# GRU inputs read back from DRAM in pairs of steps and turned by VectorE in blocks, instead of turned group by group by TensorE

## The reference

```
# layer 0, attention over T = 32, 16 heads of 16
scale, shift = split(cond @ W_emb + b_emb)
xn  = rms_norm(x, g_norm) * (1 + scale) + shift
q, k, v = heads(xn @ W_qkv);  q, k = rms_norm(q, g_q), rms_norm(k, g_k)
o   = softmax(q k^T / 4) v
x2  = x + o + o @ W_out
# layer 1, GRU over time, first state h = cond
gi = x2[:, t] @ W_ih + b_ih;  gh = h @ W_hh + b_hh
r, z = sigmoid(gi_r + gh_r), sigmoid(gi_z + gh_z)
n = tanh(gi_n + r * gh_n);  h = (1 - z) * n + z * h
out[:, t] = x2[:, t] + h
```

## Time and profile before

| | |
|---|---|
| median of 3 runs | 342.4 us (342.23, 342.4, 343.04) |
| span of the profiled execution | 340.0 us |
| busy: PE, DVE, ACT, POOL | 323.3, 246.3, 238.0, 224.5 us |
| attention, then seam, then GRU | to about 180, 180 to 195, from 195 us |
| granted TensorE clock | 1.00 in all slices |

### The profile page before, as it was taken

The page is one execution under the profiler, slowest core; times in us unless marked ns, Lnnn a source line. Parts: engine busy times, 40 slices in busy tenths (PEclk is TensorE's granted clock), DMA queues, the critical chain, the costliest instruction groups (busy, mean ns, idle before and its releaser), DMA issues.

```text
span 340.0 us, 12168 instructions
## 1 busy us (share of the span) xinstructions
PE 323.3 (95%) x4177; PEld 293.4 (86%) x4177; DVE 246.3 (72%) x665; ACT 238.0 (70%) x722; POOL 224.5 (66%) x404
## 2 busy tenths in 40 slices
PE   8988899899999999999986999999999999999994
PEld 8767788788888888888874999999999999999994
DVE  3778898888999999999996455565555556555555
ACT  4787777778888788889656566666666666666662
POOL 6787787867777877878778346555555555555542
PEclk9999999999999999999999999999999999999999
DMA  5965237742343333233332221111112111122221
GB/s 202 307 193 151 86 76 234 226 132 85 109 121 113 101 114 99 86 117 116 112 109 65 80 77 48 61 49 62 62 62 62 48 58 50 62 62 62 63 62 33
DMA packets 32205, 34.14 MB, mean 100 GB/s; under 512 B 5286, under 2 KB 26796, under 8 KB 32172
## 3 DMA queue, kind: packets, MB, share of 16 engines
q1 hardware_dynamic: 25868, 26.10, 25.6%
q10 hardware_dynamic: 6304, 7.61, 7.0%
HBM read 12.46 MB, written 8.39 MB: 61 GB/s over the span
## 4 chain that ended last, share of the span: by engine, by line
PE 78%; POOL 7%; SPq 4%; DMA 4%; issue 3%; DVE 3%; ACT 1%; POOLq 0%; DVEq 0%; ACTq 0%
PE bank L1287 38%; PE bank L1244 19%; PE bank L1400 4%; PE bank L1419 4%; PE bank L1388 4%; DMA operands<-operands 4%; PE bank L1531 3%; SPq L414 2%; POOL operands L485 2%; PE bank L1380 2%; SPq L405 2%; PE bank L1250 2%; PE bank L1371 2%; POOL xn L496 1%; POOL xn_lo L531 1%
## 5 line engine op out<-in xcount | busy, mean ns | idle before, releaser
L1287 PE MATMUL bank<-wih_lo,wo_parts 128*128 128x256 f32 x192 | 56.2, 294 | 0.0
L1287 PE MATMUL bank<-wih_hi,wo_parts 128*128 128x256 f32 x192 | 54.6, 285 | 0.2 <-POOL pair_lo L600 0.2
L1287 PE MATMUL bank<-wih_hi,pair_lo 128*128 128x256 f32 x192 | 52.8, 279 | 0.0
L1287 PE MATMUL bank<-wqkv_hi,hT_hi 128*128 128x256 f32 x192 | 52.5, 292 | 0.0
L611 POOL TENSOR_TENSOR operands<-operands,h 128x128 f32<-128x128 f32 x64 | 29.6, 462 | 34.2 <-ACT operands L932 33.4
L1287 PE MATMUL bank<-wqkv_lo,hT_hi 128*128 128x256 f32 x192 | 49.9, 279 | 0.0
L1187 DVE TENSOR_TENSOR operands<-bank,operands 128x128 f32<-128x128 f32 x64 | 18.6, 291 | 39.3 <-ACT operands L929 39.3
L1244 PE MATMUL bank<-wqkv_hi,xn_hi 128*128 128x512 f32 (+1 forms) x124 | 46.4, 375 | 0.2 <-POOL xn_lo L531 0.2
L618 POOL TENSOR_TENSOR w_emb_sb<-h,w_emb_sb 128x256 f32<-128x256 f32 x31 | 22.9, 737 | 30.7 <-DVE h L1204 30.7
L1287 PE MATMUL bank<-wqkv_hi,hT_lo 128*128 128x256 f32 x192 | 42.7, 279 | 0.0
L1244 PE MATMUL bank<-wqkv_hi,xn_lo 128*128 128x512 f32 (+1 forms) x124 | 41.9, 338 | 0.0
(11 more groups left out here) (138 smaller groups left out, 975.2 us busy)
## 6 DMA issues: line engine op xcount, KB each, us to landing
v_diag<-v_rows SPq DMA_DIRECT2D x124, 34.0 KB, 2.1
operands<-operands SPq DMA_DIRECT2D x32, 128.0 KB, 2.1
out_dram<-x ACTq DMA_DIRECT2D x16, 256.0 KB, 2.6
w_emb_sb<-out_dram SPq DMA_DIRECT2D x32, 128.0 KB, 2.1
operands<-operands SPq DMA_DIRECT2D x63, 64.0 KB, 2.0
out_dram<-w_emb_sb SPq DMA_DIRECT2D x31, 128.0 KB, 1.7
x_in<-in_x_dram SPq DMA_DIRECT2D x7, 512.0 KB, 8.6
stage_w<-in_L_cond_W_ih_dram ACTq DMA_DIRECT2D x2, 384.0 KB, 3.4
```

The costliest lines, as they stand in the source:

```text
L1287: return pe.matmul(dst, moved, gate_columns(weights, k, block), start=False, stop=True, skip_group_check=True)
```

## The change: what it does, and the diff

Only groups 24 to 31 are still turned by TensorE, and only their first two steps are kept (`late_x2T`, 4 x 32 columns). Everything else comes back from DRAM: for each pair of steps SyncE issues four DMAs, one for each quarter of the features, that put x2 with the group on 32 partitions of each quarter (`load_quarters`; runs of 64 features, 256 bytes). VectorE turns the 128x512 tile in 32x32 blocks (`turned_quarters`), even and odd features apart, and GpSimd makes the high and low parts from it, its reads being strided now (`turned_pair`). The features so come in another order, and the rows of w_ih are loaded in that order. The weights' tile is no longer shared by pair_hi. The last two groups are stored by SyncE instead of ScalarE. For pair 0 the quarters of groups 0 to 23 are loaded ahead of the end of attention.

```diff
+FIRST_TURNED = 24
-        x2T = sb("x2T", [P, KC * T * B])
+        late_x2T = sb("late_x2T", [P, 2 * KC, NTURNED * GB])
+        x_quarters = sb("x_quarters", [P, 2, 2 * D])
+        x_turned = sb("x_turned", [P, 2, 2 * D])
+        def turned_pair(slot):
+            return x_turned[:, slot, :].rearrange("p (i n g) -> p n g i", i=GB, n=2 * KC)
+        def by_parity(slot):
+            return x_quarters[:, slot, :].rearrange("p (n f c) -> p n c f", n=2 * GB, c=KC)
 # SyncE
+            def load_quarters(pair, slot, groups):
+                n = 2 * pair
+                rows = out[groups.start * GB:groups.stop * GB, bass.ds(n, 2), :]
+                for f in range(4):
+                    sp.dma_start(x_quarters[PB * f + groups.start:PB * f + groups.stop, slot, :],
+                                 rows[:, :, f * QF:f * QF + QF]).then_inc(quarters_loaded[slot], 16)
+            for stored in x2_stored:
+                sp.wait_ge(stored, 16 * (NG // 4 - early_stores))
+            load_quarters(0, 0, early)
+            sp.wait_ge(x2_ready, NG)
+            sp.dma_start(out.rearrange("(g b) t d -> (b t) g d", b=GB)[:, NG - 2:NG, :], x2[:, 2:4, :])\
+              .then_inc(x2_stored[1], 16)
             for stored in x2_stored:
                 sp.wait_ge(stored, 16 * (NG // 4))
+            def next_quarters(pair, slot):
+                sp.wait_ge(quarters_turned, pair - 1)
+                load_quarters(pair, slot, slice(0, NG))
+            load_quarters(1, 1, slice(0, NG))
+            load_rows(0, 0)
+            load_rows(1, 1)
+            next_quarters(2, 0)
...
 # GpSimd
-            pool.wait_ge(x2T_ready, NG)
+            pool.wait_ge(quarters_turned, 1)
+            pool.tensor_copy(by_group(pair_hi[:, 0, :, :])[:, :, early, :], turned_pair(0)[:, :, early, :])\
+                .then_inc(early_high, 1)
...
             def high_pair(u, slot):
-                pool.tensor_copy(pair_hi[:, slot, :, :], x2T_pair(u)).then_inc(pair_hi_ready, 1)
+                pool.wait_ge(quarters_turned, u + 1)
+                pool.tensor_copy(by_group(pair_hi[:, slot, :, :]), turned_pair(slot)).then_inc(pair_hi_ready, 1)
 # ScalarE
-                    result(d)
+                    if later(d, FIRST_TURNED) and isinstance(d, int):
+                        result(d)
+                rows = source[(i % KC) * P:(i % KC) * P + P, :]
+                if i < KC:
+                    rows = source.rearrange("(f c) n -> c f n", c=KC)[i]
 # VectorE
+                if turn_is(base, u, NG - 1 + DVE_PT):
+                    dve.wait_ge(quarters_loaded[0], 64)
+                    dve.transpose(x_turned[:, 0, :], by_parity(0)).then_inc(quarters_turned, 1)
...
+            def turned_quarters(pair, slot, loads):
+                dve.wait_ge(quarters_loaded[slot], 64 * loads)
+                if later(pair, 3):
+                    dve.wait_ge(pair_lo_ready, pair - 1)
+                dve.transpose(x_turned[:, slot, :], by_parity(slot)).then_inc(quarters_turned, 1)
             # in step, ahead of reset_state(0):
+                if isinstance(t, int) and t == 0:
+                    turned_quarters(1, 1, 1)
+                if s % 2 == 1 and has_pair(base, (s + 3) // 2):
...
 # TensorE
-                if d is not None and not late_result:
+                if isinstance(d, int) and d >= FIRST_TURNED and not late_result:
                     result_transposes(d, (u - PE_X2T) % 4)
...
+            pe.wait_ge(early_high, 1)
             pe.wait_ge(first_pair_hi, 1)
```

More of the change, by code:

```diff
@@ L261, in adaptive_attention_gru @@
         x2T_ready = sem("x2T_ready")
+        quarters_clear = sem("quarters_clear")
+        quarters_loaded = [sem(f"quarters_loaded{i}") for i in range(2)]
+        quarters_turned = sem("quarters_turned")
+        early_high = sem("early_high")
+        early_low = sem("early_low")
         rz_ps = [sem(f"rz_ps{c}") for c in range(KC)]
@@ L346, in has_pair, with by_group @@
             return not isinstance(base, int) or base // 2 + n < T // 2
[L348 to L352, removed]
+        early, late, last_group = slice(0, FIRST_TURNED), slice(FIRST_TURNED * GB, B - GB), slice(B - GB, B)
+        late_rows, last_rows = slice(0, (NTURNED - 1) * GB), slice((NTURNED - 1) * GB, NTURNED * GB)
+        def turned_pair(slot):
+            return x_turned[:, slot, :].rearrange("p (i n g) -> p n g i", i=GB, n=2 * KC)
+        def by_parity(slot):
+            return x_quarters[:, slot, :].rearrange("p (n f c) -> p n c f", n=2 * GB, c=KC)
+        def by_group(pair):
+            return pair.rearrange("p n (g i) -> p n g i", i=GB)
         turn = [0]
@@ L446, in store_rows, with rows @@
                 sp.dma_start(out[:, t, :], x2_rows[:, s, :]).then_inc(out_done[s], 16)
-            def rows(q, s):
+            def next_quarters(pair, slot):
+                sp.wait_ge(quarters_turned, pair - 1)
+                load_quarters(pair, slot, slice(0, NG))
+            def rows(q, s, quarters=True):
                 store_rows(q * 4 + s, s)
@@ L453, in rows @@
                     load_rows(q * 4 + s + 2, (s + 2) % 4)
-            for t in range(4):
-                load_rows(t, t)
+                if isinstance(q, int) and q == 0 and s == 0:
+                    next_quarters(3, 1)
+                if quarters and s % 2 == 1:
+                    next_quarters(q * 2 + (s + 7) // 2, (s + 7) // 2 % 2)
+            load_quarters(1, 1, slice(0, NG))
+            load_rows(0, 0)
+            load_rows(1, 1)
+            next_quarters(2, 0)
+            load_rows(2, 2)
+            load_rows(3, 3)
             for s in range(4):
                 rows(0, s)
-            with sp.Fori(1, T // 4 - 1) as q:
+            with sp.Fori(1, T // 4 - 2) as q:
                 for s in range(4):
                     rows(q, s)
+            for s in range(4):
+                rows(T // 4 - 2, s, False)
             for s in range(2):
-                rows(T // 4 - 1, s)
+                rows(T // 4 - 1, s, False)
             store_rows(T - 2, 2)
@@ L1098, in residual @@
                 if later(o, 4):
-                    dve.wait_ge(x2T_ps, o - 3)
+                    if isinstance(o, int) and o >= FIRST_TURNED + 4:
+                        dve.wait_ge(x2T_ps, o - 3 - FIRST_TURNED)
                     dve.wait_ge(x2_stored[slot // 2], (o - slot) * 4)
@@ L1304, in input_term @@
                 part, weights = ((pair_hi, wih_hi), (pair_hi, wih_lo), (pair_lo, wih_hi))[term]
-                return add_product(input_block(e, block), part[:, pair_slot, k, e * B:e * B + B], weights, k, block)
+                return add_product(input_block(e, block), part[:, pair_slot, e * KC + k, :], weights, k, block)
             def unread_products(tiles, count):
@@ L1376, in result_transposes @@
                 pe.wait_ge(v_ready, capped(d, PE_X2T - PE_V + (1 if isinstance(d, int) and d in LATE_RESULTS else 0)))
-                if later(d, 1):
-                    pe.wait_ge(x2T_ready, d)
+                if d > FIRST_TURNED:
+                    pe.wait_ge(x2T_ready, d - FIRST_TURNED)
                 for c in range(KC):
-                    last = pe.transpose(p_x2T[:, c * P:c * P + P], x2[:, slot, c * P:c * P + P], ident[:, :])
+                    last = pe.transpose(p_x2T[:, c * P:c * P + P],
+                                        x2[:, slot, :].rearrange("p (f c) -> p c f", c=KC)[:, c], ident[:, :])
                 last.then_inc(x2T_ps, 1)
```

61 lines of the change are left out of this document (36 added, 25 removed).

## The result

The changed kernel takes 352.28 us (median of 4 runs, 351.68 to 353.52) against 342.31 us before: a ratio of 1.0295, 95% interval 1.0267 to 1.0323. It is slower, as predicted, but by twice the amount: the forecast was 347.0 us, and the measured time lies above the upper end of the range, 349.8. A second set of 6 runs on another chip gave 350.21 us and 1.0245 (1.0195 to 1.0295), its median just over that end too. The profiled execution took 351.68 us with a span of 349.9 us. One execution of the kernel before (440.88 us), one of experiment 5 (357.58 us) and one of the repeat of experiment 6 (354.41 us, the profiled one) ran over 1.5% longer than the fastest of their kernel at a lower granted clock, and no median, ratio or reading here uses them.

The account below looks back on a forecast made before the run. TensorE was taken as the bound, with 78% of the chain of waits. Span 340.0 - 3.7 (attention) + 1.0 and 5.8 (seam) + 1.6 (clock) = 344.7 us, plus 2.4 to the median, taken as 347.0 us; range 343.0 to 349.8.

Parts of the forecast that it names:

- it can grow by 0.7 us unseen: Steady GRU: GpSimd's low part of 1.30 us, followed by z*h, could lengthen by 0.7 us at no cost.
- the steady GRU: GRU steps behind the seam: block transposes, more DMAs and strided reads cost nothing, within 0.2 us.
- GpSimd pays for strides: Rival, chance 0.05: GRU low parts at double cost make z*h 0.5 us late per pair, 7.5 us; 356 us.
- The seam, first place: Turn of the pair 0 blocks ahead of oT(30), behind the quarters' loads: +1.0 us, ends 0 and 2.
- the sum: Whole kernel: 340.0 - 3.7 + 1.0 + 5.8 + 1.6 = 344.7 us of span; median 347.1, taken as 347.0 us.
- Attention: Removed result transposes shorten turns that TensorE sets by 0.22 us: gain 3.7 us, ends 3.3 and 5.3.
- VectorE becomes the bound: Rival, chance 0.07: in attention VectorE's 4.72 us of work leave 0.11, half of the gain goes; 349 us.
- Step 0: Seam, second place: GRU step 0 waits for the last store, then pair 1's loads: +5.8 us, ends 4.3 and 7.
- The clock: TensorE, idle near 6 us before h, restarts step 1 at half pace: +1.6 us, ends 0 and 3.3.
- Clock kept: Rival, chance 0.30: the same seam, but TensorE's clock does not fall; 345.4 us.
- Not slower: Rival, chance 0.12: ahead of step 0, pair 1's quarters are in by 195.4 us; 341.4 us.

Follow-up runs that it names:

- experiment 5: Changed kernel with pair 0 turned after oT(31), pairs 1 and 2 turned in steps 1 and 2, and strides on VectorE's write: 345.41 us, 1.0055.
- experiment 6: Changed kernel with 36 unread products on TensorE ahead of its wait for h(0): 349.58 us, 1.0272; on the other chip 349.19 us, 1.0220.
- experiment 3: Changed kernel with the strides moved from GpSimd's reads to VectorE's transpose write: 348.51 us, 1.0179.
- experiment 4: Kernel before, with GpSimd's high and low parts of pairs 1 and up reading in strides of 256 bytes, nothing else: 345.51 us, 1.0136.
- experiment 1: Changed kernel with VectorE's block transpose of pair 0 behind oT(31) instead of ahead of oT(30): 351.01 us, 1.0266.
- experiment 8: Changed kernel with the 24 pairs of result transposes of groups 0 to 23 back on TensorE, unread: 355.35 us, 1.0441.
- experiment 2: Changed kernel with the turn and the high and low parts of pairs 1 and 2 one step later: 352.67 us, 1.0284.
- 10: Changed kernel with pairs 0 and 1 made early, strides on VectorE's write, and pair 1's turn and parts moved later: 338.68 us, 0.9892.

## Why the prediction was wrong

**The step that failed:** "it can grow by 0.7 us unseen", of GpSimd's low part in the steady GRU. I had checked it against z*h of the next step alone. Its first reader is TensorE, which wants it for the next inputs ahead of h; there the slack is next to nothing already in the kernel before. So the term that I had at nothing, the steady GRU, was +2.38 us. The growth itself was in my rival "GpSimd pays for strides", with the wrong reader and so the wrong price (half a microsecond over a bound of 0.7, 7.5 us in all, chance 0.05). Measured: 1.30 us became 1.58, +22%, the copy 0.61 became 1.13, +84%, and the steady steps lost 2.4 us; with plain reads (experiment 3) that loss was gone, and with strides alone (experiment 4) it was there. The Trainium skill (GPSIMD Engine Reference, 7. Performance pitfalls for Q7 kernels) gives such reads 50% more. Here the copy had 84% and the subtraction 22%, so the measurement decides.

**The seam, first place:** right mechanism, mis-sized, +2.15 us against +1.0. Counted from scores 31, oT(30) came 2.98 us later (the wait of 2.27 and the transpose of 0.71), where I had 2.0: the four issues took 3.40 us, where I had taken the 2.84 of the earlier trace rows, and landed about 1 us later than I had it. The slack behind it was 0.8 us, near the 1.0 of the sum. Experiment 1 took 1.96 us away.

**Attention:** right mechanism, mis-sized: -2.56 us in this profile against -3.7. Of the 1.1 us that are missing, 0.64 are the late start of this profile, which is chance and no effect of the change. The other 0.5 lie up to turn 15, where scores waited 1.40 and 1.42 us for keys and I had let half of the gain through; from there to scores 31 the gain was 3.48 us, against my 3.5. The mean over ten profiles is -3.0, and single ones differ by 3 us. The rival "VectorE becomes the bound" is out: a turn of 4.85 us is what TensorE's slots give (5.05 less 0.22 is 4.83), VectorE has 0.12 us to spare in it, and with the transposes back (experiment 8) the turn is 5.06 us again.

**Step 0:** right, +6.29 against +5.8, by the steps I had named: store, four loads, block transpose, high and low part, z*h. The strides took 0.45 + 0.22 us of it, where I had 0.3.

**The clock:** right, +1.59 against +1.6, and shown by experiment 6. The Trainium skill (TensorE: Matmul & The Clock Gate, HAM oscillation) describes a TensorE that waits for DMAs and comes back at half clock. This trace agrees, with 0.50 behind a wait of 6.18 us for h, which stood behind DMAs. "Clock kept" is out.

**The sum:** the four misses are 2.4 + 1.15 + 1.1 + 0.5 = 5.2 us; 347.0 + 5.2 = 352.2 against 352.28. All went to the same side. Without the 0.64 us of chance in attention's the kernel would still lie above the range. "Not slower" fell where I had put its point of decision: the quarters of pair 1 landed at 196.9 us (197.3 in the old trace's frame, by residual 31), not by 195.4.

## What to carry to other kernels

When an operation on a side engine grows, list every reader of its result and take the earliest one in program order; a multiplication issued half a step ahead is easily missed, and moving work to "one step later" fails for the same reason. Where a transposed or regrouped tile must be strided on one side, put the stride on the engine with slack. A round trip through DRAM that starts with the last store of a stage belongs to that stage's critical path, so give the first items that need it another source.

## What the runs showed of the hardware

- GpSimd's cost of a strided source differs by operation: the 128x512 copy went from 0.61 to 1.13 us, the two-input subtraction from 1.30 to 1.58 (strides of 512 bytes) and to 1.57 (256 bytes).
- VectorE's block transpose of 128x512 took 0.705 us with a plain write and 1.115 us with a strided one.
- The clock fell to 0.50 behind a wait of TensorE's of 3.35 us as well as behind one of 6.18 us. It also fell (0.66 to 0.77 in a stretch of 5 us) between 180 and 190 us in the profiles of experiments 2, 3, 5 and 10, in the others read here not. In three of them the stage to residual 31 is 1.5 us longer than in their counterparts (11.97 against 10.4, 9.91 and 9.90 against 8.45), in experiment 2's it is not (10.15). Runs of the changed kernel differ by about as much (351.68 to 353.52 us); that the clock is the reason is not shown, nor what decides it.
- The first input tile let ScalarE start between 5.95 and 6.87 us from one profile to the next; differences below 1 us in where attention begins are no effect of an edit.
